# Expert rows of three routers made for all tiles at once, and one weight split moved from a mixing loop into the attention before it

## The reference

```python
x = x + attention_l(layernorm(x), context)
x = x + ffn_l(layernorm(x))
```

```python
topv, topi = top_k(softmax(x @ router), 2)            # layers 1 and 3
w = zeros(N, E).at[arange(N)[:, None], topi].add(topv / sum(topv))
out = einsum('ner,eor->no', h * w[:, :, None], B)   # h: the low-rank rows
```

## Time and profile before

| what | value |
|---|---|
| median of 3 runs | 2166.19 us (2165.17 to 2166.44) |
| span of the profiled execution | 2159.1 us, 39910 instructions |
| TensorE busy | 1995.0 us, 92% |
| VectorE busy | 1587.5 us, 74% |
| ScalarE busy | 1335.2 us, 62% |
| GpSimd busy | 204.8 us, 9% |
| mean granted TensorE clock | 0.972 |

### The profile page before, as it was taken

One profiled execution on the slowest core, in us unless ns is written; L12 is line 12 of the kernel. 1 busy time (PEld: TensorE's weight loads), 2 busy tenths in 40 slices (PEclk: granted clock), 3 DMA queues, 4 the chain that ended last, 5 costly groups with the idle time before them and its releaser, 6 DMA issues.

```text
span 2159.1 us, 39910 instructions
## 1 busy us (share of the span) xinstructions
PE 1995.0 (92%) x13920; PEld 1147.6 (53%) x13920; DVE 1587.5 (74%) x4091; ACT 1335.2 (62%) x3897; POOL 204.8 (9%) x207
## 2 busy tenths in 40 slices
PE   4887999999999999999976797999999999999778
PEld 2554444466666666666643464444555555555444
DVE  6666555677777777777768576767798889988773
ACT  3665212287777777777753565434788888888621
POOL 3674000000000000000000463000000000000020
PEclk8899999999999999999998998999999999999999
DMA  5231111224444544453530331111044333343200
GB/s 215 62 55 16 59 59 40 78 58 95 108 81 91 110 85 91 81 114 74 95 79 20 74 69 36 59 69 49 16 93 92 71 90 93 62 90 83 62 6 39
DMA packets 318935, 157.65 MB, mean 73 GB/s; under 512 B 309648, under 2 KB 309648, under 8 KB 311312
## 3 DMA queue, kind: packets, MB, share of 16 engines
q1 hardware_dynamic: 318736, 155.09, 31.2%
HBM read 77.44 MB, written 2.10 MB: 37 GB/s over the span
## 4 chain that ended last, share of the span: by engine, by line
PE 59%; DVE 26%; ACT 8%; issue 4%; DMA 1%; POOL 1%; SPq 0%; ACTq 0%; DVEq 0%; POOLq 0%
PE bank L702 54%; ACT hid L1628 4%; DVE hid L2221 3%; DVE masked L2180 3%; DVE negmax L2184 2%; DVE wa_lo L1746 2%; DVE x L2193 2%; DVE oT_lo L2211 2%; DVE negmax_n L1920 1%; DVE wo_lo L1746 1%; ACT bd_hi L1505 1%; PE bank L794 1%; PE bank L810 1%; PE bank L811 1%; DVE xnT_lo L1813 1%
## 5 line engine op out<-in xcount | busy, mean ns | idle before, releaser
L702 PE MATMUL bank<-xnT_hi,wa_hi 128*128 128x512 f16 x736 | 279.1, 379 | 4.2 <-PE bank L702 1.8
L702 PE MATMUL bank<-xnT_hi,wa_lo 128*128 128x512 f16 x736 | 279.1, 379 | 0.0
L702 PE MATMUL bank<-xnT_lo,wa_hi 128*128 128x512 f16 x736 | 279.1, 379 | 0.0
L702 PE MATMUL bank<-wo_hi,oT_hi 128*128 128x512 f16 x576 | 221.5, 385 | 28.2 <-DVE oT_lo L2211 27.2
L2221 DVE SCALAR_TENSOR_TENSOR hid<-probs,inv_total,hid 128x256 f16<-128x256 f32 (+1 forms) x512 | 179.9, 413 | 81.4 <-ACT hid L1628 81.4
L702 PE MATMUL bank<-wo_hi,oT_lo 128*128 128x512 f16 x576 | 221.4, 384 | 0.0
L702 PE MATMUL bank<-wo_lo,oT_hi 128*128 128x512 f16 x576 | 221.2, 384 | 0.0
L702 PE MATMUL bank<-wa_hi,xnT_hi 128*128 128x512 f16 (+3 forms) x640 | 203.1, 323 | 6.7 <-DVE hid L1882 2.6
L702 PE MATMUL bank<-wa_lo,xnT_hi 128*128 128x512 f16 (+3 forms) x640 | 203.0, 323 | 0.0
L702 PE MATMUL bank<-wa_hi,xnT_lo 128*128 128x512 f16 (+3 forms) x640 | 202.9, 323 | 0.0
L1587 ACT ACTIVATE probs<-bank,negmax,rms_r 128x256 f32<-128x256 f32 x256 | 140.9, 560 | 96.3 <-DVE negmax L2177 96.3
(11 more groups left out here) (252 smaller groups left out, 4860.3 us busy)
## 6 DMA issues: line engine op xcount, KB each, us to landing
raw<-in_w_qkv_dram SPq DMA_DIRECT2D x18, 1536.0 KB, 7.0
raw<-in_w_out_dram SPq DMA_DIRECT2D x18, 1024.0 KB, 5.3
raw<-in_w_ffn_dram SPq DMA_DIRECT2D x15, 1024.0 KB, 4.9
pT<-hid SPq DMA_TRANSPOSE x256, 3.1
raw<-in_w_ffn0d_dram SPq DMA_DIRECT2D x7, 512.0 KB, 3.5
x<-in_x_dram SPq DMA_DIRECT2D x4, 512.0 KB, 5.5
expert_b<-in_expert_b_dram SPq DMA_DIRECT2D x1, 2048.0 KB, 9.4
kT<-k SPq DMA_TRANSPOSE x128, 2.4
```

The lines of the kernel that those rows point to most:

```text
L702: mm = pe.matmul(dst, l, r, start=start and k == 0, stop=stop and k == n - 1)
```

## The change

The constant ROUTED2 and the last router's number grow by 2, since each router has one `route_link` more. In the router, sixteen instructions on one tile each become four on all tiles: two compare the expert numbers with the chosen ones, two multiply by the gates. The pieces of `w_qkv2` go from the mixing loop into the last two units of the first wide attention (two pieces each); by the rules of the code VectorE makes their low parts in steps 63 and 64, and the load of the first weights of feed-forward 2 (`w_ffn2`, 0) is issued by SyncE after unit 63 instead of after the mixing loop's splits.

```diff
-ROUTED2 = 19
+ROUTED2 = 21
@@ wide_pieces
+    if n == 0 and s >= UNITS - 2:
+        return [(NUMBER["w_qkv2", 0], 2 * (s - UNITS + 2)), (NUMBER["w_qkv2", 0], 2 * (s - UNITS + 2) + 1)] if s < UNITS else []
@@ mix on ScalarE
-                    if n == 0 and b < PIECES:
-                        high(NUMBER["w_qkv2", 0], b)
@@
-            router(2, 16, 64, 21)
+            router(2, 16, 64, 23)
@@ router on VectorE
-                for b in range(B):
-                    dve.tensor_scalar(pick_a[:, b, 0:E], c("iota")[:, 0:E], topf[:, b, 0:1], gates[:, b, 0:1],
-                                      ALU.is_equal, ALU.mult)
-                    op = dve.tensor_scalar(pick_b[:, b, 0:E], c("iota")[:, 0:E], topf[:, b, 1:2], gates[:, b, 1:2],
-                                           ALU.is_equal, ALU.mult)
+                places = c("iota")[:, 0:E].unsqueeze(1).broadcast_to([P, B, E])
+                for k, pick in enumerate((pick_a, pick_b)):
+                    op = dve.tensor_tensor(pick[:, :, 0:E], places, topf[:, :, k].unsqueeze(2).broadcast_to([P, B, E]),
+                                           ALU.is_equal)
+                route_link(op)
+                for k, pick in enumerate((pick_a, pick_b)):
+                    op = dve.tensor_tensor(pick[:, :, 0:E], pick[:, :, 0:E],
+                                           gates[:, :, k].unsqueeze(2).broadcast_to([P, B, E]), ALU.mult)
                 route_link(op)
@@ mix on VectorE
-                    if n == 0 and b < PIECES:
-                        low(NUMBER["w_qkv2", 0], b)
```

## The result

The changed kernel takes 2156.45 us (median of 5 executions, 2155.71 to 2159.33) against 2165.17 us (2162.42 to 2166.44) for the kernel before beside it: ratio 0.9963, 95% interval 0.9952 to 0.9974. It is faster, as forecast, but by more: 2160.0 us was forecast and 2157.3 us was the low end of the range.

The account below looks back on a forecast made before the run. TensorE was taken to bound the long stages, with VectorE the chain in short stretches between. Savings 2.4 + 1.3 + 0 + 2.5 + 0 = 6.2 us from 2166.2 gave 2160.0 us, range 2157.3 to 2163.6.

Parts of the forecast that it names:

- The picks: First router: sixteen VectorE instructions become four, 3.23 us shrink to 0.85, saving 2.4 us, between 2.2 and 2.45.
- Router 2: Before the second feed-forward's experts: the earlier route closes TensorE's 1.33 us gap ahead of expert 6, worth 1.3 us.
- Router 3: Last router: TensorE's base projection covers VectorE's work by 4 us, so the cheaper picks are worth 0.
- Part 3: Splits placed in units 62 and 63 fit idle time of ScalarE and VectorE: cost 0, or 3.4 us without cover.
- The mixing loop: Taking w_qkv2's splits out of the loop saves 2.5 us; upper bound 3.9, lower bound 0.4.
- The walk through VectorE's order: Loop without splits: VectorE waits for TensorE 1.0, then 0.35 to 0.7 us; tile 4's low part 2.3 to 2.6 us earlier.
- rival B: Everything comes off: all 3.9 us in the loop count, a stretch behind gets the high clock, 0.5; 2158.1 us; chance 0.12.
- I take these 7.1 us as unchanged and subtract from the median: Whole kernel: the median 2166.19 stands 7.1 us above the profiled span 2159.1; savings are subtracted from that median.
- I allow 1 us either way and count 0: TensorE behind idle stretches: shifts may move a few matmuls between clock levels; 1 us either way allowed, 0 counted.
- A: Mixing loop: TensorE stays at the low clock and takes over, split removal gives only 0.4 us; 2162.1 us; chance 0.16.
- C: Units 62 and 63: late splits stretch both softmax tails, 8.4 us lost against 6.2 won; 2168.4 us; chance 0.06.
- D: Routers: picks get no cheaper, broadcast operands at 0.8 us each eat 3.2 of 3.23 us; 2163.7 us; chance 0.06.

Follow-up runs that it names:

- half changes: Two kernels, each with one part of the change against the kernel before: only the router picks (2159.01 us), only the moved w_qkv2 split (2163.11 us).
- the picks alone: Changed kernel with the w_qkv2 split put back into the mixing loop, only the router picks changed: 2159.01 us, ratio 0.9973 to the kernel before.
- the splits alone: Changed kernel with the old sixteen picks per router, only the w_qkv2 split moved: 2163.11 us, ratio 0.9988 to the kernel before.
- the fillers of the last set: Changed kernel plus unread TensorE matmuls in the first router, behind the mixing loop and in both wide attentions' last two units: 2150.79 us, repeated 2150.12 us.

## Why the prediction came out wrong

**Part by part the mechanism held.** The picks: forecast 2.4 us in the first router, measured 2.44. Router 2: 1.3 against 1.34, with the gap at expert 6 gone, and shown to be the picks' by the two half changes. Router 3: 0; the base projection's 16.14 us are unchanged. From the third router's logits to the end the kernel before takes 81.8 us and the picks alone 81.6, both at a mean granted clock of 0.95, although the route comes 2.2 us earlier; the changed kernel's 80.2 come at 0.98. Part 3: 0; the reciprocal is still led by ScalarE's last sum, 0.03 us behind it as before, with about 0.1 us of room where I had 0.05, and the four splits in one place bear out the threshold.

**The mixing loop was 0.2 us short.** I had 2.5, measured were 2.73. The walk through VectorE's order met the first five tiles (6.13 us, forecast 6.0 to 6.4, waits of 0.96 and 0.41 where I had 1.0 and 0.35 to 0.7). What it left out is the tail, 0.25 us: in the kernel before the second fall made VectorE wait 0.17 us for TensorE near 1171.5, and without the splits that fall doesn't come. This is the smaller part of rival B (a stretch that gets the high level).

**The step that failed is the base and the clock.** "I take these 7.1 us as unchanged and subtract from the median" set the trace of one execution against the median of three others. In every execution with a listed span the own time is 1.7 to 1.9 us above it, so the profiled execution of before had taken some 2160.9 us, 4 below the kernel's median of 58: the 7.1 were 1.8 of overhead and 5.3 of spread. The median of three was itself too high a base. The same text then said of the clock "I allow 1 us either way and count 0". But 21 executions of the changed kernel show 14 us between the fastest and the slowest, 58 of the kernel before show 11, and a single stretch is worth 2.6 by itself.

The miss in medians, 2160.0 to 2156.45, is 3.6 us: the base 1.1 (2166.19 of three, 2165.1 of 58), the terms 0.3 (6.51 for 6.2), the first five executions of the changed kernel 0.5 below its 21, and 1.7 that no stretch accounts for. By the means this rest is 1.1 us (7.6 against 6.5), with 1.5 either way, so it can't be told from nothing.

**What makes the spread.** The traces show it as TensorE's clock. In all twelve, two long stretches without a fall, one in each wide attention, take the same time to 0.1 us, 729.2 and 458.4, whatever the kernel. The stretches that differ have the same instructions at another clock. From layer 3's last `negmax` to the third router's logits, for instance, in the second and third trace of the changed kernel and in the one with fillers behind the mixing loop (time, TensorE's busy time and matmuls, and, after the five engines, the granted clock):

```profile
2039.11:2068.00 28.89, 18.61 (x158) 11.74 (x158) 25.67 (x53) 11.35 (x30) 11.00 (x8) 0.94 0.05 10
```

```profile
2047.69:2077.74 30.05, 19.95 (x158) 12.12 (x158) 25.88 (x53) 11.35 (x30) 11.03 (x8) 0.89 0.05 10
```

```profile
2043.08:2074.76 31.68, 22.53 (x158) 13.18 (x158) 25.88 (x53) 11.35 (x30) 11.01 (x8) 0.78 0.05 9
```

The same 158 matmuls take 28.89, 30.05 and 31.68 us at 0.94, 0.89 and 0.78.

For the executions without a trace only the mean granted clock is known, and it is a rough measure. Within one kernel the time falls by about 0.8 us per 0.001 of it (0.5 to 1.0 by kernel). The changed kernel's mean is 0.9749 against 0.9724, worth 2.0 us, and at equal clock it is 5.6 us faster (0.8 either way), the picks alone 4.9 (1.0) and the splits alone 1.2 (0.9). These stand 0.9 below, 1.1 above and 1.5 below their stretches, for which I have no cause. The profiled execution of before is off the line too: at 0.972 other executions of that kernel took 2164.4 to 2169.5 us, this one about 2160.9. So that the rest of the miss is the clock is likely and not shown, and no run here sets where a fall lands. The Trainium skill, "TensorE: Matmul & The Clock Gate", Part 1, says that the hardware watches TensorE's activity on a free-running clock of its own and doesn't count instructions. By that rule one kernel meets it at another phase each time. The three traces of the unaltered changed kernel agree in kind, with falls in other places; no run here shows the phase itself.

**The rivals.** A (the loop stays at the low level): refuted, the third tile is at the high level. B (everything comes off, 2158.1): its 3.9 us in the loop do not come off in the change; with filler they nearly do (18.94 to 15.31 us, 3.63). Its number was the nearest by luck: the base and the draw moved the total, not its 3.9. C (late splits in units 62 and 63): refuted by the half changes, and real once four stand in one place. D (dear picks): refuted, 0.22 us each.

## What to carry over

Before a sum of small terms is set against a median, learn how far executions of the unaltered kernel lie apart and what overhead its span has; a few microseconds read off from stretches can be right to 0.3 us while the total moves by several more. A block of work moved from a VectorE-bound loop into another engine's idle time costs nothing up to the exact length of VectorE's gap and shows in full beyond it. Where the spread comes from TensorE's clock falling behind short idle stretches, multiplying for nobody in those stretches is worth trying: here filling four places gave 7.2 us, as much again as the change, while filling the first one or two gave nothing that the total could show.

## What the runs showed of the hardware

- The same kernel ran between 2149.99 and 2164.07 us, with the same instructions and the same waits, and its three traces (spans 2148.2, 2154.7 and 2157.9 us) differ in which stretches TensorE passed at 1.2 instead of 2.4 GHz. With the fillers of the last set ten executions lay within 5 us, the first five within 1.8.
- 46 filler matmuls of 256 columns ahead of the loop kept its granted clock at 1.00, and 12 to 20 per gap did so at the end of the wide attention; the page counts 14128 matmuls and as many weight loads with all of them, 13920 of each in the kernel before. I saw no cost of theirs on the other engines (VectorE's loop was as fast or faster).
- Most of the twelve output-projection matmuls of unit 63 (4.16 against 2.39 us from the first's start to the last's) and the few matmuls ahead of them (1.63 against 1.08) at the low level make up 2.3 of the 2.6 us between 33.3 and 35.9; which of the two a run gets differed with nothing changed in the kernel.
- One and the same stretch of 158 matmuls took 28.89, 30.05 or 31.68 us at a mean granted clock of 0.94, 0.89 or 0.78, while two stretches of 729.2 and 458.4 us without a fall agreed to 0.1 us in all twelve traces.
- A comparison with two broadcast operands on 128x64 cost no more on VectorE than one with a single broadcast operand, 0.22 us, and where no link stood between two of them the second started 0.14 us behind the first.
